# First layer of a two-layer graph kernel: TensorE takes its steps in pairs, scores of two, then values of two

## The reference, cut to what matters

```
h = max(layernorm(x), 0)
q, k, v = h Wq.T + bq, h Wk.T + bk, h Wv.T + bv        # 4 heads of 64
scores  = clip(q k.T / 8, -10, 10), -10 where adj == 0 # per head, 8 chunks of 256 keys
ctx     = sum over chunks of softmax(scores in the chunk) v_chunk
out     = layernorm(ctx Wo.T + bo + h) * gamma + beta
x       = x + out
```

## Time and profile before

| | |
|---|---|
| median of 3 runs | 4495.8 us (4494.7 to 4496.92) |
| the profiled execution | 4492.85 us, span of its instructions 4491.0 us |
| first layer | the first 3010 us of the span |
| mean granted TensorE clock | 0.992 of full speed |
| busy: PE, DVE, ACT, POOL | 4246.6, 4024.7, 2977.8, 714.7 us |

### The profile page before, as it was taken

The page is one execution under the profiler, slowest core; times in us unless marked ns, Lnnn a source line. Parts: engine busy times, 40 slices in busy tenths (PEclk is TensorE's granted clock), DMA queues, the critical chain, the costliest instruction groups (busy, mean ns, idle before and its releaser), DMA issues. The chain is left out here.

```text
span 4491.0 us, 168889 instructions
## 1 busy us (share of the span) xinstructions
PE 4246.6 (95%) x72733; PEld 3492.7 (78%) x72733; DVE 4024.7 (90%) x9728; ACT 2977.8 (66%) x3317; POOL 714.7 (16%) x613
## 2 busy tenths in 40 slices
PE   7999999999999999999999999969999999999998
PEld 5777777677677777777767777758999999999998
DVE  5998899889898899889988989978999999999998
ACT  5555555555555555555555555538999999999997
POOL 3121122112121122112211211110000010000100
PEclk9999999999999999999999999989999999999999
DMA  5100110011001010011011101113212122122221
GB/s 122 58 23 19 34 30 21 26 30 30 26 21 30 21 35 23 24 31 30 21 27 29 30 21 27 36 35 102 76 39 83 41 70 81 31 80 54 58 71 36
DMA packets 174046, 188.95 MB, mean 42 GB/s; under 512 B 7520, under 2 KB 157408, under 8 KB 173152
## 3 DMA queue, kind: packets, MB, share of 16 engines
q1 hardware_dynamic: 166192, 159.49, 12.8%
q0 software_dynamic: 7088, 18.36, 1.7%
HBM read 110.43 MB, written 38.03 MB: 33 GB/s over the span
## 5 line engine op out<-in xcount | busy, mean ns | idle before, releaser
L789 ACT ACTIVATE slot<-slot,shift 128x1024 f32<-128x1024 f32 x1024 | 1113.5, 1088 | 1184.5 <-PE slot L639 1176.2
L651 PEld LDWEIGHTS outs<-v_s,probs 128*64 128x64 f32 x32768 | 1042.2, 137 | 450.5 <-issue 271.3
L925 DVE SCALAR_TENSOR_TENSOR probs<-slot,bound 128x1024 f32<-128x1024 f32 x1024 | 1245.6, 1217 | 90.1 <-ACT slot L789 84.7
L651 PE MATMUL outs<-v_s,probs 128*64 128x66 f32 x32768 | 1179.5, 225 | 62.7 <-DVE ctx_sum L945 58.1
L1559 ACT ACTIVATE u<-s_all,d_sign 128x1024 bf16<-128x1024 f32 x1024 | 1117.7, 1139 | 57.0 <-PE sums L1460 39.1
L638 PE MATMUL slot<-q_hl,k_hl 128*128 128x512 f32 x2048 | 919.7, 449 | 59.1 <-DMA q_hl<-q_hl 35.9
L639 PE MATMUL slot<-q_hl,k_hl 128*128 128x512 f32 x2048 | 812.6, 397 | 0.0
L945 DVE SCALAR_TENSOR_TENSOR ctx_sum<-outs,inv,ctx_sum 128x64 f32<-128x64 f32 x3584 | 769.6, 278 | 31.7
L1456 PE MATMUL sums<-x_mixed,u 128*128 128x130 f16 x8192 | 785.7, 219 | 1.7 <-issue 1.5
L1460 PE MATMUL sums<-x_mixed,mask 128*128 128x65 f16 x8192 | 759.2, 193 | 4.6 <-issue 4.5
L1691 DVE TENSOR_TENSOR u<-u,mask 128x1024 f16<-128x1024 bf16 x1024 | 687.1, 681 | 76.8 <-ACT u L1559 68.2
(11 more groups left out here) (156 smaller groups left out, 3667.3 us busy)
## 6 DMA issues: line engine op xcount, KB each, us to landing
q_hl<-q_hl SPq DMA_DIRECT2D x128, 256.0 KB, 3.6
s_all<-s_turned SPq DMA_DIRECT2D x64, 512.0 KB, 5.6
x_q_s<-in_x SPq DMA_DIRECT2D x32, 512.0 KB, 5.1
x<-y SPq DMA_DIRECT2D x32, 512.0 KB, 3.2
t_o_s<-x SPq DMA_DIRECT2D x16, 1024.0 KB, 5.7
out<-t_o_s SPq DMA_DIRECT2D x16, 1024.0 KB, 6.7
x_q_s<-x SPq DMA_DIRECT2D x28, 512.0 KB, 6.1
probs<-in_adj POOLq DMA_DIRECT2D x12, 512.0 KB, 7.0
```

Of the source, the lines that this page charges most:

```text
L651: end = nc.tensor.matmul(outs[i % OUTS][rows_of, q, 0:V_COLS], probs[:, i % PROBS, r, q * P + g * D:q * P + (g + 1) * D], v_s[:, c * JC + ...
L789: nc.scalar.activation(slot[:, :, :], slot[:, :, :], ACT.Exp, bias=shift[:, 0:1], scale=SCALE).then_inc(act_done, 1)
L925: nc.vector.scalar_tensor_tensor(probs[:, i % PROBS, :, :], spot(kind, "step", s, i)[:, :, :], P_LOW, bound[:, (i // H) % 2, :, :], ALU.ma ...
```

## The change

TensorE's order within a strip of the first layer is written anew. Scores are issued step by step; after each odd step from 3 on come the values of two steps, i-3 and i-2. So the order is S0 S1 S2 S3 V0 V1 S4 S5 V2 V3 and so on to S30 S31 V28 V29; then V30 and V31 follow. The next strip's first scores are no longer taken ahead of V31: they come after it, at the head of the next strip. The queries of steps 30 and 31 keep their places behind S30 and S31, so V28 now comes behind S31 and q1. In a batch's last strip the two `keys` stand before V30 and V31, in place of V29 and V30. No other engine's code, no wait, no buffer and no instruction is changed; only the order on TensorE is.

```diff
                 for s in range(NS):
                     has_before = s > 0 or not first
-                    for i in range(STEPS + LAG):
+                    for i in range(STEPS):
                         if i == TURN_AT and has_before:
...
-                        if i < STEPS and not (i == 0 and s > 0):
-                            scores(s, i)
-                        if i == STEPS + LAG - 1 and s < NS - 1:
-                            scores(s + 1, 0)
+                        scores(s, i)
                         if i in t_pairs(s) and not last:
...
-                        if STEPS - 1 <= i < STEPS - 1 + Q_USES:
-                            qu = i - (STEPS - 1)
-                            if s == NS - 1 and not last:
-                                keys(0, qu, used(b, kind, "t", 0, 1), used(b, kind, "k", 0, qu), spot(kind, "k", 0, qu))
-                        if i >= LAG:
-                            values(s, i - LAG)
+                        if i % 2 == 1 and i >= 2 * LAG - 1:
+                            values(s, i - 2 * LAG + 1)
+                            values(s, i - 2 * LAG + 2)
+                    for i in range(STEPS - LAG, STEPS):
+                        if s == NS - 1 and not last:
+                            qu = i - (STEPS - LAG)
+                            keys(0, qu, used(b, kind, "t", 0, 1), used(b, kind, "k", 0, qu), spot(kind, "k", 0, qu))
+                        values(s, i)
```

## The result

The changed kernel takes 4538.5 us in the median of 4 runs (4536.39 to 4543.09) against 4496.4 us (4494.7 to 4497.06) before: a ratio of 1.0096, with an interval from 1.0078 to 1.0113. It is 42 us slower; 40 us were forecast. The profiled execution took 4539.79 us (span 4538.0, mean granted clock 0.985 instead of 0.992).

The account below looks back on a forecast made before the run. VectorE was taken to pace most of a strip, TensorE the short steps and, with mutual waits, the seam. Terms +22, 0, +3 and +15 gave +40 us: 4533 us profiled, 4536 for the median; range 4503 to 4563.

Parts of the forecast that it names:

- Step (a): Within strips: pairing saves TensorE 0.35 us a pair, but VectorE's pace hides most; -0.5 us a strip, between 0 and -1.0.
- Step (b): Inner seams: VectorE waits for V28 and S0; net of pairing +0.7 us at 16 seams, +1.4 at 8, +22 us.
- the 2.6 to 3.0 named as the sign: Sign of being right: TensorE waits 2.6 to 3.0 us before V31 for scale 29 at each inner seam.
- the 0.3 us that was to be won back on the way to project: Next strip's head, S2 to project: one pair takes TensorE 4.1 us instead of 4.43, cutting the 1.47 us delay by 0.3.
- The sum of the order alone: Forecast without more clock falls: seams net of pairing +22 us, plus +3 for the last batch's last strip, +25 us.
- Step (c): Batches' last strips: 0 for moved keys; +3 us in the last batch, where VectorE waits for later values, between 0 and 10.
- Step (d): Inner seams: the wait before V31 drops TensorE's clock at 19 of 24, 1.0 us each; +15 us net, bounds 0 and +28.
- the one with the seam and no falls: Rival: seam costs as forecast, clock falls no more often than now; +25 us, 4520 us, chance 0.20.
- the falls inside strips: Rival: TensorE's waits come once in two steps, twice as long, and its clock falls inside strips; 4568 us, chance 0.08.
- the faster case: Rival: TensorE's shorter pair gives it a lead and VectorE's waits before clips go; -30 us, 4465 us, chance 0.12.
- the cancelling one: Rival: strip middles win their whole 1.0 us a strip and the clock stays; +9 us or less, around 4500, chance 0.10.

Follow-up runs that it names:

- experiment 3: Changed kernel with pairs only to step 29, then the earlier kernel's seam order; last batch's last strip in single steps: 4473.4 us, ratio 0.9955 to before.
- experiments 6: Kernel before, in single steps, with VectorE's scale cut to one 0.42 us instruction in every step (sum over chunks left out): 4402.8 us, ratio 0.9794 to before.
- experiment 7: Changed kernel, in pairs, with VectorE's scale cut to one 0.42 us instruction in every step (sum over chunks left out): 4317.6 us, ratio 0.9603 to before.
- experiment 5: Changed kernel with V28 put ahead of q1 again, S0 still after V31: 4512.8 us, ratio 1.0035 to before.
- experiment 1: Changed kernel with the next strip's first scores ahead of V31 again: 4496.8 us, ratio 1.0005 to before.
- experiment 4: Changed kernel with five unneeded matmuls between V30 and V31 at each of the 24 seams: 4524.8 us, ratio 1.0070 to before.
- Experiments 2: Kernel before, in single steps, with the next strip's first scores moved after V31: 4523.1 us, ratio 1.0062 to before.

## Why the prediction was right

Step (a), pairs: -0.5 us a strip was forecast; experiment 3 against before shows -0.45 to -0.5, won for the most part in the short steps, as the forecast has it. That VectorE's pace hides the rest is shown by experiments 6 and 7.

Step (b), the seam: forecast +0.7 us for the 16 ordinary strips and +1.4 for the 8 first ones, net of (a). Undisturbed strips of the middle batches show +0.88 and +0.67, and +1.65; in the first and the last batch it is less. The two causes named stand apart by experiment: V28 behind q1 costs 0.5 us, 1.3 in a first strip (experiment 5), S0 behind V31 costs 0.4 to 1.2 (experiment 1 against the changed kernel; 0.4 in a third strip, where S0 taken ahead waits 2.0 to 2.3 us for its copy). The two don't simply add: against experiment 3, with both back, a first strip differs by 2.1 us, where the single ones give 1.2 and 1.3. The wait before V31 was forecast as 2.7 us, from a V30 that ends at 1349.2 in one place and 1349.4 in another; it is 2.50, just under the 2.6 to 3.0 named as the sign, and 2.8 in a batch's first strip. Of the 0.3 us that was to be won back on the way to project, 0.14 came. The sum of the order alone was +25 with (c); experiment 4, in which the clock holds at the seams, is 31 us over before, some 28 without its extra work. In its trace the first layer alone is 19.9 us over before; without the extra work, and with some 4 us added for the four falls that the kernel before has, the order comes to about 22.

Step (c): the last strip, +3 forecast, is 2.3 us longer in the changed kernel, with a fall of the clock in that strip before and after. The cause is the one named: VectorE's waits before inverts there, for TensorE's values, rise from 1.9 to 15.6 us, and its waits before clips fall from 10.9 to 0.3. The other last strips are unchanged but for one, 1.7 us longer, beside a fall.

Step (d), the clock: forecast 19 falls of 1.0 us, +15 net of those before. There were 15, most of them of 1.1 to 2.3 us; the share is 12 to 14 us by the totals of experiment 4, and by the strips of its trace 23 us, some 19 net of those before. The count was too high and the price too low, and the two errors cancelled in part. That the term comes out near 15 is luck: it was counted from the length of the wait alone, which the runs don't bear out (see the last section).

The range's lower end is 9 us over 4496, which is 4505 and not 4503; nothing hangs on it. Of the rivals, the one with the seam and no falls is experiment 4; the falls inside strips did not come; the faster case would have needed a shorter step on VectorE, which is experiment 7; the cancelling one did not come, and gain and loss cancel only with S0 ahead again (experiment 1).

## What to carry to other kernels

Ask first which engine's step the distance between settled steps equals; an order that makes another engine's steps cheaper is worth only that first engine's waits, here 0.5 us of an 84 us strip and not the 5 us that TensorE could save in it. When an order is written anew, walk its seams instruction by instruction: an early first piece of the next round fills a wait that no other useful work in this order fills, and losing it cost more than the whole pairing won. Take the two apart before judging: pairs with the old seam are 0.45% faster than before, pairs with the new seam 0.96% slower.

## What the runs showed of the hardware that was not expected

A wait of TensorE of 2.5 to 2.8 us was followed by the half clock (0.50) at 15 of 24 seams and not at the others, at the same place in the program and after waits as long. In some of them the fall began before the wait had ended, so that V31 itself ran at the low level: the 32 matmuls at 1826.15 took 2.03 us instead of 1.15.

```profile
1826.15 2.03 PE L651 MATMUL outs<-v_s,probs 128*64 128x66 f32 x32 [2.51 <-DVE ctx_sum L944]
```

The length of the wait alone does not tell how often the clock falls. Experiments 2 and 5 both wait 2.11 us before V31 at the second and third seams of the six middle batches; the clock fell at 1 of these 12 in experiment 2 and at 7 in experiment 5. Over all 24 inner seams it was 5 and 17, and 3 in experiment 7, which issues in pairs too and waits 2.07 or 2.4 us. Each count is of one execution; what decides is open.

Five useless matmuls (ten rows in the profile) in that wait kept the clock at full at all 24 seams and made the kernel about 12 us faster in the total.
